# First cross attention: keys stacked by DMA, two score products per head; the experts' low parts on VectorE

## The reference

```python
# layer 0, cross attention: 16 heads of 64; keys from 2048 context rows and the 128 latents
kv = concat([layernorm(ctx) @ Wkv, ln @ Wkv])        # k, v: 16 heads
qn = rmsnorm(q, qn_g) * 64 ** -0.5
kn = rmsnorm(k, kn_g)
sim = einsum('bhid,bhjd->bhij', qn, kn)               # 128 queries x 2176 keys, a head
out = softmax(sim) @ v
# layer 0, experts: 16 experts, 512 -> 1024 -> 512, the best two for each of 512 tokens
p = softmax(x @ Wr + br); keep the two largest, normalised
y = sum over the two of p_e * (gelu(x @ W1[e] + b1[e]) @ W2[e] + b2[e])
```

## Time and profile before

| | |
|---|---|
| median of 3 runs | 2880.97 us (2880.17 to 2882.69) |
| profiled execution, its own time | 2885.5 us |
| its span | 2883.5 us |
| busy: TensorE, VectorE, ScalarE, GpSimd | 85%, 66%, 55%, 33% of the span |
| low parts of the exponents, L544, GpSimd | 272 of 1161 ns |
| low parts of the down weights, L1345, GpSimd | 23 of 4486 ns, 103.2 us |
| low parts of the up weights, L1432, VectorE | 46 of 2622 ns |
| low parts of the down weights, L1437, VectorE | 23 of 2281 ns |

### The profile page before, as it was taken

One profiled execution on the slowest core, in us unless ns is written; L12 is line 12 of the kernel. 1 busy time (PEld: TensorE's weight loads), 2 busy tenths in 40 slices (PEclk: granted clock), 3 DMA queues, 4 the chain that ended last, 5 costly groups with the idle time before them and its releaser, 6 DMA issues. The chain is left out here.

```text
span 2883.5 us, 56810 instructions
## 1 busy us (share of the span) xinstructions
PE 2461.0 (85%) x21666; PEld 1580.6 (55%) x21666; DVE 1896.8 (66%) x4120; ACT 1599.7 (55%) x2934; POOL 950.5 (33%) x727
## 2 busy tenths in 40 slices
PE   4489999999999999998687779987389999997786
PEld 2235555555555656665335467764266767675342
DVE  4578777777777776665144289996477777763226
ACT  3336666666666665555223278865347777777113
POOL 2312333333433342223100023333446766656000
PEclk9699999999999999999888789998699999997787
DMA  3311121112111110000251179984543434221301
GB/s 119 99 32 41 34 77 46 34 38 78 52 34 38 47 52 5 5 3 5 84 216 63 40 280 349 336 300 143 169 146 111 130 110 131 81 85 42 118 1 75
DMA packets 201502, 277.29 MB, mean 96 GB/s; under 512 B 49408, under 2 KB 128128, under 8 KB 200336
## 3 DMA queue, kind: packets, MB, share of 16 engines
q1 hardware_dynamic: 197280, 265.54, 27.8%
q10 hardware_dynamic: 3312, 6.03, 0.5%
q0 software_dynamic: 640, 2.10, 0.3%
HBM read 225.51 MB, written 48.10 MB: 95 GB/s over the span
## 5 line engine op out<-in xcount | busy, mean ns | idle before, releaser
L544 POOL TENSOR_TENSOR a_plo<-a_p,a_phi 128x512 bf16<-128x512 f32 x272 | 315.9, 1161 | 817.5 <-ACT a_phi L600 816.8
L734 PE MATMUL ps<-w_hi,a_xhi 128*128 128x512 bf16 x1088 | 416.0, 382 | 0.4 <-DVE a_v L623 0.4
L735 PE MATMUL ps<-w_lo,a_xhi 128*128 128x512 bf16 x1088 | 416.0, 382 | 0.0
L736 PE MATMUL ps<-w_hi,a_xlo 128*128 128x512 bf16 x1088 | 415.1, 382 | 0.0
L1927 POOL TENSOR_TENSOR a_plo<-a_p,a_phi 128x512 bf16<-128x512 f32 x256 | 303.4, 1185 | 191.8 <-ACT a_phi L1964 184.5
L566 ACT ACTIVATE a_kraw<-ps 128x256 f32<-128x256 f32 x272 | 104.5, 384 | 412.2 <-PE ps L736 410.4
L623 DVE TENSOR_TENSOR a_v<-ps,a_v 128x256 bf16<-128x256 f32 x272 | 114.9, 422 | 261.5 <-ACT a_v L568 260.0
L2039 DVE CUSTOM_DVE_ANT_0 a_junk<-ps,a_biasrow 128x512 bf16<-128x512 f32 x256 | 176.2, 688 | 115.8 <-PE ps L2144 114.7
L1959 ACT ACTIVATE a_p<-ps,a_mcol 128x512 f32<-128x512 f32 x256 | 175.2, 684 | 101.0 <-PE ps L2162 94.8
L596 ACT ACTIVATE a_p<-ps,a_mcol 128x512 f32<-128x512 f32 x256 | 175.5, 686 | 57.2 <-PE ps L787 57.1
L668 DVE CUSTOM_DVE_ANT_0 a_junk<-ps,a_mrow 128x512 bf16<-128x512 f32 x256 | 174.7, 682 | 13.3 <-PE ps L765 12.9
(11 more groups left out here) (437 smaller groups left out, 7204.3 us busy)
## 6 DMA issues: line engine op xcount, KB each, us to landing
e_wst<-in_L_ffn_W SPq DMA_DIRECT2D x46, 2048.0 KB, 9.8
a_xn<-in_ctx SPq DMA_DIRECT2D x16, 1024.0 KB, 5.5
a_ct<-in_ctxT SPq DMA_DIRECT2D x16, 1024.0 KB, 5.4
a_ks<-k1h_d SPq DMA_DIRECT2D x128, 128.0 KB, 2.5
k1h_d<-a_khi SPq DMA_DIRECT2D x64, 128.0 KB, 2.3
k1l_d<-a_klo SPq DMA_DIRECT2D x64, 128.0 KB, 1.7
a_ks<-k1l_d SPq DMA_DIRECT2D x64, 128.0 KB, 2.7
xh_d<-a_xshi SPq DMA_DIRECT2D x48, 128.0 KB, 1.8
```

Of the source, the lines that this page charges most:

```text
L544: pool.tensor_tensor(p_lo[:, m % 3, :], p32[:, m % 2, :], p_hi[:, m % 3, :], ALU.subtract)\
L734: pe.matmul(out, x_hi[:, c, tile], w_hi[:, c, g, :], start=(c == 0), stop=False)
L735: pe.matmul(out, x_hi[:, c, tile], w_lo[:, c, g, :], start=False, stop=False)
L736: last = pe.matmul(out, x_lo[:, c, tile], w_hi[:, c, g, :], start=False, stop=(c == C - 1))
```

## The change

First cross attention. High and low part of one head are stacked on the 128 partitions: 64 rows of one, 64 of the other, in ks, [128 partitions, 2 units, 4 heads, 2176 keys]. ScalarE and VectorE write the transposed keys into small rings of three groups (k_hi, k_lo), and SP issues four transfers from there into ks for each turn. q_both holds the high part of a head's queries on both halves of the partitions, q_low the low part on those rows where ks has the key's high part, with zeros on the others. A tile's scores are then, for each of four heads, ks with q_both (hi*hi + lo*hi) and ks with q_low (hi*lo), 128 columns each. The maximum's product uses ks and q_both too, so it takes the low part of the keys in. It waits for the transfers and stands a step later (e + 5 instead of e + 4). The ring of values has 28 instead of 29 slots.

Experts. Both halves of the down weights' low part are made on VectorE, the second after the result's copy. The selection of the overflow tiles takes one comparison, after eight small instructions ahead of the loop that find for each token its place in each overflow tile.

```diff
-    k_hi = sb("a0_khi", [P, 2, 2, S0], BF16)
-    k_lo = sb("a0_klo", [P, 2, 2, S0], BF16)
+    ks = sb("a0_ks", [P, 2, 4, S0], BF16)
+    KR = 3
+    k_hi = sb("a0_khi", [P, KR, 512], BF16)
+    k_lo = sb("a0_klo", [P, KR, 512], BF16)
...
-    VR = 29
+    VR = 28
...
-    qb_hi = sb("a0_qbhi", [P, 3, 2, 256], BF16)
-    qb_lo = sb("a0_qblo", [P, 3, 2, 256], BF16)
+    q_both = sb("a0_qboth", [P, 3, 4, P], BF16)
+    q_low = sb("a0_qlow", [P, 3, 4, P], BF16)
...
-    qb_in = [sem("a0_qb_in0"), sem("a0_qb_in1"), sem("a0_qb_in2")]
+    q_in = [sem("a0_q_in0"), sem("a0_q_in1"), sem("a0_q_in2")]
+    ks_in = [sem(f"a0_ks_in{j}") for j in range(KR)]
...
                 for h in range(4):
-                    k_max[e + 4 + h].append((u, j, h))
+                    k_max[e + 5 + h].append((u, j, h))
...
-        if j < 4:
-            return k[:, u % 2, pr, j * 512:(j + 1) * 512], ps[:, KT, :]
-        return k[:, u % 2, :, S2:S0], ps[:, KT, 0:2 * P].rearrange("p (r n) -> p r n", n=P)
+        w = 512 if j < 4 else 2 * P
+        return k[:, turn_index(u, j, pr) % KR, 0:w], ps[:, KT, 0:w]
...
+    def stack_uses(u, j, pr):
...
+        return 64 * (turn_index(u, j, pr) // KR)
...
-                    for src, dst in ((t["q_hi_d"], qb_hi), (t["q_lo_d"], qb_lo)):
-                        sp.dma_start(dst[r, u % 3, :, half * P:half * P + P], src[b, r, 2 * g:2 * g + 2, :])\
-                          .then_inc(qb_in[u % 3], 16)
+                    for z in range(2):
+                        sp.dma_start(q_both[64 * z:64 * z + 64, u % 3, half:4:2, :], t["q_hi_d"][b, r, 2 * g:2 * g + 2, :])\
+                          .then_inc(q_in[u % 3], 16)
+                    sp.dma_start(q_low[r, u % 3, half:4:2, :], t["q_lo_d"][b, r, 2 * g:2 * g + 2, :])\
+                      .then_inc(q_in[u % 3], 16)
...
+            def stack(u, j, pr):
+                x = turn_index(u, j, pr)
+                if u >= 2:
+                    sp.wait_ge(s_mm, NT0 * (u - 2) + min(4 * j + 4, NT0))
+                for k, done, swap in ((k_hi, kthi_done, 0), (k_lo, ktlo_done, 1)):
+                    sp.wait_ge(done, x + 1)
+                    for half in range(2):
+                        z = half ^ swap
+                        src = k[64 * half:64 * half + 64, x % KR, :]
+                        if j < 4:
+                            sp.dma_start(ks[64 * z:64 * z + 64, u % 2, 2 * pr + half, j * 512:(j + 1) * 512], src)\
+                              .then_inc(ks_in[x % KR], 16)
+                        else:
+                            sp.dma_start(ks[64 * z:64 * z + 64, u % 2, half:4:2, S2:S0],
+                                         src[:, 0:2 * P].rearrange("p (r n) -> p r n", n=P)).then_inc(ks_in[x % KR], 16)
...
-            sp.wait_ge(zero_done, 2)
+            sp.wait_ge(zero_done, 1)
...
+                for u, j, pr in k_turn[n]:
+                    stack(u, j, pr)
...
-            pool.memset(qb_hi[:], 0.0).then_inc(zero_done, 1)
-            pool.memset(qb_lo[:], 0.0).then_inc(zero_done, 1)
+            pool.memset(q_low[:], 0.0).then_inc(zero_done, 1)
...
-                if u >= 2:
-                    act.wait_ge(s_mm, NT0 * (u - 2) + min(4 * j + 4, NT0))
+                if stack_uses(u, j, pr):
+                    act.wait_ge(ks_in[turn_index(u, j, pr) % KR], stack_uses(u, j, pr))
...
                 if j == 0 and h == 0:
-                    pe.wait_ge(qb_in[u % 3], 64 * (u // 3 + 1))
-                pe.wait_ge(ktlo_done, turn_index(u, j, h // 2) + 1)
+                    pe.wait_ge(q_in[u % 3], 96 * (u // 3 + 1))
+                pr = h // 2 if j < 4 else 0
+                pe.wait_ge(ks_in[turn_index(u, j, pr) % KR], stack_uses(u, j, pr) + 64)
...
                 if j < 4:
-                    mm = pe.matmul(out, qb_hi[:, u % 3, h // 2, (h % 2) * P:(h % 2 + 1) * P],
-                                   k_hi[:, u % 2, h // 2, j * 512:(j + 1) * 512], start=True, stop=True)
+                    mm = pe.matmul(out, q_both[:, u % 3, h, :], ks[:, u % 2, h, j * 512:(j + 1) * 512],
+                                   start=True, stop=True)
...
                     for i in range(4):
-                        mm = pe.matmul(out[:, i * P:(i + 1) * P],
-                                       qb_hi[:, u % 3, i // 2, (i % 2) * P:(i % 2 + 1) * P],
-                                       k_hi[:, u % 2, i // 2, S2:S0], start=True, stop=True)
+                        mm = pe.matmul(out[:, i * P:(i + 1) * P], q_both[:, u % 3, i, :], ks[:, u % 2, i, S2:S0],
+                                       start=True, stop=True)
...
-                for pr in range(2):
-                    o = out[:, pr * 256:(pr + 1) * 256]
-                    pe.matmul(o, k_hi[:, u % 2, pr, tile], qb_hi[:, u % 3, pr, :], start=False, stop=False)
-                    pe.matmul(o, k_hi[:, u % 2, pr, tile], qb_lo[:, u % 3, pr, :], start=False, stop=False)
-                    last = pe.matmul(o, k_lo[:, u % 2, pr, tile], qb_hi[:, u % 3, pr, :], start=False, stop=(pr == 1))
+                for h in range(4):
+                    o = out[:, h * P:(h + 1) * P]
+                    pe.matmul(o, ks[:, u % 2, h, tile], q_both[:, u % 3, h, :], start=False, stop=False)
+                    last = pe.matmul(o, ks[:, u % 2, h, tile], q_low[:, u % 3, h, :], start=False, stop=(h == 3))
...
-    ds = sb("e_ds", [P, 2, B], F32)
-    G2 = sb("e_gm2", [P, B, P], BF16)
+    dso = sb("e_dso", [P, OVER, B], F32)
+    ds2 = sb("e_ds2", [P, OVER, B], F32)
+    first = sb("e_first", [P, OVER, B], F32)
+    base = sb("e_base", [P, OVER], F32)
...
-    w1hi, w1lo, w2hi, w2lo_a, w2lo_b = sem("e_w1hi"), sem("e_w1lo"), sem("e_w2hi"), sem("e_w2loa"), sem("e_w2lob")
+    w1hi, w1lo, w2hi, w2lo = sem("e_w1hi"), sem("e_w1lo"), sem("e_w2hi"), sem("e_w2lo")
...
-                    sp.wait_ge(w2lo_a, q - 1)
-                    sp.wait_ge(w2lo_b, q - 1)
+                    sp.wait_ge(w2lo, 2 * (q - 1))
...
-            for q in range(TILES):
-                pool.wait_ge(w2hi, 2 * q + 2)
-                pool.tensor_tensor(half(w_lo, q, 1, 1), half(wst, q, 1, 1), half(w_hi, q, 1, 1), ALU.subtract)\
-                    .then_inc(w2lo_b, 1)
...
-            def down_low(q):
-                dve.wait_ge(w2hi, 2 * q + 1)
-                dve.tensor_tensor(half(w_lo, q, 1, 0), half(wst, q, 1, 0), half(w_hi, q, 1, 0), ALU.subtract)\
-                   .then_inc(w2lo_a, 1)
+            def down_low(q, i):
+                dve.wait_ge(w2hi, 2 * q + i + 1)
+                dve.tensor_tensor(half(w_lo, q, 1, i), half(wst, q, 1, i), half(w_hi, q, 1, i), ALU.subtract)\
+                   .then_inc(w2lo, 1)
...
-                if q < E:
-                    dve.tensor_tensor(G[:, q % 2], places, dms[:, :, q].unsqueeze(2).to_broadcast([P, B, P]),
-                                      ALU.is_equal).then_inc(g_ready, 1)
-                else:
-                    step(dve.tensor_scalar(ds[:], d12[:], -(P * q + 1.0), None, ALU.add))
-                    dve.tensor_tensor(G[:, q % 2], places, ds[:, 0].unsqueeze(2).to_broadcast([P, B, P]), ALU.is_equal)
-                    step(dve.tensor_tensor(G2[:], places, ds[:, 1].unsqueeze(2).to_broadcast([P, B, P]), ALU.is_equal))
-                    dve.tensor_tensor(G[:, q % 2], G[:, q % 2], G2[:], ALU.add).then_inc(g_ready, 1)
+                place_in = dms[:, :, q] if q < E else dso[:, q - E, :]
+                dve.tensor_tensor(G[:, q % 2], places, place_in.unsqueeze(2).to_broadcast([P, B, P]), ALU.is_equal)\
+                   .then_inc(g_ready, 1)
...
+            step(dve.tensor_scalar(base[:], ramp[:, 0:OVER], float(P), E * P + 1.0, ALU.mult, ALU.add))
+            by_tile = base[:].unsqueeze(2).to_broadcast([P, OVER, B])
+            step(dve.tensor_tensor(dso[:], d12[:, 0].unsqueeze(1).to_broadcast([P, OVER, B]), by_tile, ALU.subtract))
+            step(dve.tensor_tensor(ds2[:], d12[:, 1].unsqueeze(1).to_broadcast([P, OVER, B]), by_tile, ALU.subtract))
+            step(dve.tensor_scalar(first[:], dso[:], -0.5, None, ALU.is_gt))
+            step(dve.scalar_tensor_tensor(first[:], dso[:], P - 0.5, first[:], ALU.is_lt, ALU.mult))
+            step(dve.tensor_tensor(dso[:], dso[:], ds2[:], ALU.subtract))
+            step(dve.tensor_tensor(dso[:], dso[:], first[:], ALU.mult))
+            step(dve.tensor_tensor(dso[:], dso[:], ds2[:], ALU.add))
...
-                down_low(q)
+                down_low(q, 0)
...
+                down_low(q, 1)
...
             def down(q):
-                pe.wait_ge(w2lo_a, q + 1)
-                pe.wait_ge(w2lo_b, q + 1)
+                pe.wait_ge(w2lo, 2 * q + 2)
...

```

## The result

The changed kernel takes 2801.66 us (median of 4 runs, 2801.26 to 2810.52) against 2881.83 before: a ratio of 0.9727, 95% interval 0.9705 to 0.9749. The forecast was 2810 us, range 2793 to 2838. The profiled execution's own time is 2801.7 us, its span 2799.9.

The account below looks back on a forecast made before the run. TensorE was taken to bound the first cross attention and VectorE the experts, at 13.15 us a tile. Attention 52 - 14 + 2.7 = 41 plus experts 30 gives 71 us, so 2881 becomes 2810, range 2793 to 2838.

Parts of the forecast that it names:

- Score tile: First cross attention: eight 128-column products replace six of 256, 0.21 us less a tile, 52 us over 247 steps.
- Waits that grow: First cross attention: TensorE's waits before key transposes and first values each grow 0.63 us a unit, 14 us lost.
- The tail: Last 25 score tiles, without projection: 0.21 us saved per pair of tiles, 2.7 us in all.
- Stacking by DMA: First cross attention: 576 new transfers on SP's queue, 3.2 us from low part to landing, hidden, cost 0 us.
- each is issued steps before its use: SP's queue in the attention: context stores, loads, queries and results behind the waiting SP are issued early; cost 0.
- the late rival: First maximum of a key group: stacked key lands late, up to 128 us per us beyond cover; chance 0.04.
- GpSimd's collisions: Experts: one VectorE instruction a tile stretches beside GpSimd's 4.08 us subtraction; removing this saves VectorE 3.3 us a tile.
- The period of 12.7: Experts: time per tile falls from 13.15 to 12.7 us, bounds 12.45 and 13.15.
- tiles 1 to 15: Experts: 14 periods of 13.09 us become 12.7, saving 5.5 us.
- 15 to 22: Experts' overflow tiles: 7 periods of 15.52 us become 12.7, saving 19.7 us.
- the end: Experts' last stretch: low-part wait shrinks by 1.8 to about 3 us, most low-clock cost returns; 4.5 us saved.
- The sum: Whole kernel: attention 41 plus experts 30 makes 71 us, from 2881 to 2810 us.

Follow-up runs that it names:

- the split products: Kernel before with each of its six 256-column score products a tile split into two of 128: 2887.5 us, ratio 1.0012.
- The subtraction for nothing: Kernel after, with GpSimd also making the second down half's subtraction into a tile nobody reads: 2875.7 us, ratio 0.9972 to the kernel before.
- one product fewer: Kernel after without the scores' product of keys and the queries' low part: 2768.3 us, ratio 0.9589 to the kernel before.

## Why the prediction was right, by its steps

- Score tile: forecast 0.21 us less, measured 0.66 to 0.45, and in units without contexts 72.5 to 68.9, 3.6 / 17 = 0.21. Right. Shown by the split products.
- Waits that grow: the places were right, the size was not quite: 0.63 each forecast, 0.50 (key) and 0.35 (values) measured on the mean. The trace shows where the differences lie. Ahead of the values one VectorE instruction of 0.46 us before is one of 0.18 after, which alone makes 0.63 - 0.28 = 0.35. Ahead of the key VectorE's run from its idle time to the low part takes 12.65 us before in the eight usual units and 12.83 in the three others, and 12.59 after in all but one: the wait grows by 0.56 and by 0.39, that is about 0.63 less what the run is shorter by. No experiment varied this alone. That the waits come from those two runs is shown: moving one instruction group out of each removed them. Over 11 units the smaller growth is 4.5 us, and 41 becomes 45.5; the trace has 45.7.
- The tail: 0.21 a pair forecast, 4.09 to 3.88. Right.
- Stacking by DMA: forecast 0 behind a cover of 5.7 us at the tightest, and 0 it was, in part by luck. Issue to landing is 2.0 us at the median (1.9 to 4.3) where 2.6 were taken. But "each is issued steps before its use" was read too kindly: two reads of contexts and the six query loads hold SP up until one key lands 9.8 us after its low part, more than the 7.4 us from which the late rival was to start. It cost nothing because the first maximum that reads that key pair comes three steps after its turn. The rival's place was right and its threshold was that of the first pair alone.
- GpSimd's collisions, 3.3 us a tile: right. VectorE's lengthened instructions before make 77.2 us over 23 tiles, 3.4 each. The subtraction for nothing shows the price: 80.0 us of lengthening, of which 72, 3.1 a tile, reach the time, as VectorE had slack in the kernel after.
- The period of 12.7: the mis-sized term. It measured 12.33, below the lower bound of 12.45. TensorE's own work is (96 + 32) x 0.0558 + 24 x 0.2158 = 12.32 start to start, so it is the only bound; the forecast had taken 12.5 from its busy time. The step that failed took, besides, a DMA share of 0.95 as 95% of a ceiling at 12.5 us; with less on TensorE the same transfers ran at 11.81 us and 379 GB/s with a share of 1.01. So the share was no limit at 0.95 or 0.99; what exactly it counts, no run here shows. By terms: tiles 1 to 15 gave 10.7 us (5.5 forecast), 15 to 22 gave 22.4 (19.7), the end 2.8 (4.5). There the wait shrank to 3.65 us and not to 3, and the last down part takes 6.67 us as before (6.64), at a granted clock of 0.78; the forecast had given back most of what the low clock costs. In all 35.9 against 30.
- The sum: 45.7 + 35.9 = 81.6 in the profiles (the medians differ by 80.2), forecast 71. The experts' period (6 us) and the smaller growth of the waits (4.5) are the missing 10.

## What to carry to other kernels

Where one engine is at 100%, count its queue from start to start and price a cut by its steady part alone; then name each wait of that engine, since an engine behind it that starts from the same event gives back what the cut saves. Those waits are worth a change of their own: moving twelve small instructions two steps and one norm a step gave another 35 us here, after the cut's 46. An instruction of another engine that stretches one of the bound's costs its full overlap, so work that takes 4.1 us on the idle engine was cheaper at 2.3 on the busy one.

## What the runs showed of the hardware

- A DMA share of 0.95 to 0.99 at 343 to 364 GB/s was no ceiling: 379 GB/s followed once the engines let buffers go earlier, and the 12.6 us that the prediction estimated as the shortest period was passed by 12.33 and 11.81. The Trainium skill (HBM Reference, Specifications (TRN2)) gives about 358 GB/s as a core's share when both cores of a pair stream, and says that one streaming alone measures well above it; this run, with one core at work, agrees: 379 GB/s over 60 us, of which 356 are loads, and up to 429 in single slices of 1.5 us.
- GpSimd is held up by VectorE as well: 5.50 us for an instruction of 4.08 that came while VectorE's was under way.
- TensorE's granted clock fell in units where more waits than usual had come together: behind waits of 2.48, 0.79 and 0.99 us it was 0.95 over the next 75 us, with 512-column products 0.43 us apart instead of 0.22 at the slow places (one product fewer).
- A query load of 64 rows in two runs of 256 bytes holds SP for 0.61 to 0.65 us. A queue in order turns six of them into 4 us for whoever stands behind.
